# Attention and a channel filter over sixteen images: one channel tile of x replaced by the sum of both

## The chip, the cores and the metric

The kernel runs on one core of one Trainium2 chip. The metric is the time of one execution in device microseconds (us), as the median of several runs. The engines are TensorE (PE, its weight loads apart as PEld), VectorE (DVE), ScalarE (ACT), GpSimd (POOL) and SyncE (SP), which issues DMAs.

## The reference

x is 16 images of 256 channels and 32 x 32 pixels. Each image goes through a self-attention block and then a filter over channels.

```python
theta = einsum('bchw,kc->bkhw', x, theta_w)            # 32 channels, 1024 pixels
phi   = pool2(einsum('bchw,kc->bkhw', x, phi_w))       # 32 channels, 256 pixels
g     = pool2(einsum('bchw,kc->bkhw', x, g_w))         # 128 channels, 256 pixels
beta  = softmax(einsum('bnk,bkm->bnm', theta, phi))    # 1024 x 256
o     = einsum('bchw,kc->bkhw', einsum('bcm,bnm->bcn', g, beta), o_w)
a     = gamma * o + x
out   = a + einsum('fc,bchw->bfhw', tpl, a)            # tpl: circulant, 27 taps over channels
```

tpl is symmetric and circulant, so 1 + tpl is one 256 x 256 matrix whose two diagonal 128 x 128 blocks are equal and whose two other blocks are equal and non-zero only in two corners of 13 channels.

## The kernel before

The 256 channels lie in two tiles of 128 partitions (t or f, 0 and 1), the pixels in two halves of 512 (h). Everything is done in fp32 precision by splitting a number into a high part that TensorE takes in its fast format (fp32r) and a low part that is the rest; `three` multiplies high by high, high by low and low by high. For one image TensorE does, for each half: the theta and phi projections (`theta_phi`, 4 matmuls of 512 columns), the g projection (`g_projection`, 6), the scores (`scores`, 4 of 256 columns), the transposed scores (`scores_transposed`, 2), attention times g (`attention_input_high` 4, `attention_input_low` 2), and the output in PSUM for each tile f: `filter_x` (three matmuls by the diagonal block of the band and one, the corner product of line 1096, by the corner of the other block with the 26 edge channels of the other tile, stacked in `x_edge`), then `add_high_attention` (2) and `add_low_attention` (1) with the weights o_w folded with the band (`w2`).

The work is pipelined over images in an order written out by hand in each engine's queue: `image(i, par)` is image 2i + par, and a queue does the last parts of that image between the first parts of the next one (ni, npar) and the loads and splits of the next but one. Every engine does its own list strictly in order and waits on semaphores. Images 0 and 1 are special cases; the rest run in a hardware loop over pairs, the last pair again written out.

VectorE's list for one image, with the lines of the profile: `sum_thetaphi` of half 0 of the next image (L709), `pool_phi` (L702), `gT_low` (L748), `theta_low` (L715), `pool_g` (L702), the sum of half 1 (L709), `pool_phi`, `split_phi` (two casts L735, one subtraction L737), `theta_low`, `pool_g`, `maxima` of half 0 (L777), `o_in_low` of half 0 (L757), `maxima` of half 1, then

```python
out_of_psum(i, par, 0, 1)
o_in_high(i, par, 1)
out_of_psum(i, par, 0, 0)
o_in_low(i, par, 1)
shifts(ni, npar)
turn_shifts(ni, npar)
for h in range(2):
    spread_shifts(ni, npar, h)
```

`out_of_psum` copies an output half tile from PSUM to `y` (L765 on VectorE, L557 on ScalarE). `shifts` (L782 and two more) makes the softmax shift from the maxima and the logarithms of the sums; `turn_shifts` (L809) transposes it and `spread_shifts` (L817) writes it into `theta_aug`, which `scores_transposed` reads.

ScalarE's list after the probabilities of an image (`probabilities_high` L542, `probabilities` L537) ends so:

```python
o_in_high(i, par, 0)
for h in range(2):
    exp_sums(ni, npar, h)
ln_sums(ni, npar)
x_high(i + 1, par, 1)
for f in (1, 0):
    out_of_psum(i, par, 1, f)
take_thetaphi_rest(i + 1, par, 0)
```

`exp_sums` (L526, four exponentials of 256 columns with a sum) waits for `maxima` of its half, `ln_sums` (L532) for nothing outside, and `shifts` on VectorE waits for `ln_sums`. `x_high` (L504) rounds a half of the next but one image. GpSimd makes the low parts: `prob_low` (L457) for both halves of the attention, the second after `theta_low` of half 1, and `x_low` (L450). SyncE loads x in halves (L306), stores y (L362) and copies the edge channels into `x_edge` (six DMAs, L332).

## Time and profile before

| | |
|---|---|
| time, median of 3 runs | 272.98 us (272.94 to 273.1) |
| profiled execution, span from first to last instruction | 271.3 us |
| PE busy | 265.4 us, 98% |
| DVE busy | 245.9 us, 91% |
| ACT busy | 243.2 us, 90% |
| POOL busy | 149.6 us, 55% |

No separate time is listed for the profiled execution. Its span is 1.7 us under the median of the runs, and that difference stands for what lies around the span. In a timeline a row gives the start, the time, the engine, the line, the operation with its shapes and how many are merged; the bracket at the end is the engine's idle time ahead of it and what ended it. Matmuls are pipelined, so the distance of two starts is what one costs.

### The profile page before, as it was taken

Reading aid. Unit: us, or ns where it says so; the run is one execution under the profiler, and the core shown is the slowest. Engines: PE = TensorE matmul, PEld = TensorE weight load, DVE = VectorE, ACT = ScalarE, POOL = GpSimd, SP = SyncE. Lnnn points to the kernel's source line nnn. Section 1 sums busy time; section 2 is a strip of 40 time slices with the busy share of each in tenths; the row PEclk is TensorE's granted clock in tenths of the full one; section 3 lists DMA queues with packets and bytes.
Section 4 is the critical chain, followed back from the end, with each engine's and each line's share of the span. In section 5 each row is a group of like instructions: output and inputs, shape, how many; then the busy total and the mean of one; then the engine's idle time right before and its main releaser. Section 6 shows DMA issues by size and latency. Waiting matters only on the chain.

```text
span 271.3 us, 4464 instructions
## 1 busy us (share of the span) xinstructions
PE 265.4 (98%) x1196; PEld 211.8 (78%) x1196; DVE 245.9 (91%) x456; ACT 243.2 (90%) x533; POOL 149.6 (55%) x79
## 2 busy tenths in 40 slices
PE   7999999999999999999999999999999999999994
PEld 3576778888888888888888888888887888888873
DVE  4998999999999999999999999999999999999953
ACT  4999999999999999998999999999999989998772
POOL 1585747574565747546673764667466475745100
PEclk9999999999999999999999999999999999999999
DMA  7978085582847657284673828467283855317044
GB/s 198 270 208 212 23 234 169 175 223 81 193 142 225 180 170 182 88 218 149 203 201 144 180 79 246 157 197 206 98 182 124 234 169 172 77 71 178 1 157 155
DMA packets 17380, 44.57 MB, mean 164 GB/s; under 512 B 2654, under 2 KB 3578, under 8 KB 16122
## 3 DMA queue, kind: packets, MB, share of 16 engines
q1 hardware_dynamic: 16682, 44.00, 56.4%
q10 hardware_dynamic: 688, 0.46, 0.5%
q8 instruction: 4, 0.07, 0.1%
q14 instruction: 6, 0.05, 0.1%
HBM read 17.45 MB, written 16.78 MB: 126 GB/s over the span
## 4 chain that ended last, share of the span: by engine, by line
PE 94%; DVE 2%; DMA 2%; ACT 0%; issue 0%; SPq 0%
PE psY L1009 10%; PE psY L988 8%; PE psY L990 7%; PE psY L989 7%; PE psV L1128 6%; PE psY L1112 6%; PE psY L1128 5%; PE psV L1112 5%; PE psV L988 3%; PE psV L990 3%; PE psV L989 3%; PE psX L1066 3%; PE psV L1096 3%; PE psV L1133 3%; PE psZ L1066 3%; PE psY L1118 3%
## 5 line engine op out<-in xcount | busy, mean ns | idle before, releaser
L457 POOL TENSOR_TENSOR prob_lo<-prob,prob_hi 128x1024 fp32r<-128x1024 f32 x30 | 72.1, 2404 | 59.7 <-ACT prob L537 32.5
L450 POOL TENSOR_TENSOR x_lo<-x_raw,x_hi 128x1024 fp32r<-128x1024 f32 x30 | 72.0, 2399 | 35.5 <-ACT x_hi L504 34.0
L504 ACT CAST x_hi<-x_raw 128x1024 fp32r<-128x1024 f32 x30 | 31.5, 1052 | 6.8 <-PE psY L1096 5.2
L526 ACT ACTIVATE psX<-psX,neg_max 128x256 f32<-128x256 f32 x60 | 26.7, 445 | 3.0 <-DVE neg_max L777 3.0
L526 ACT ACTIVATE psZ<-psZ,neg_max 128x256 f32<-128x256 f32 x60 | 27.4, 468 | 0.0
L709 DVE TENSOR_TENSOR thetaphi<-psY,thetaphi_rest 64x512 f32<-64x512 f32 x30 | 20.5, 682 | 3.8 <-ACT thetaphi_rest L508 3.1
L988 PE MATMUL psY<-x_hi,g_hi_w 128*128 128x512 f32 x56 | 22.2, 396 | 0.0
L990 PE MATMUL psY<-x_hi,g_lo_w 128*128 128x512 f32 x56 | 22.0, 393 | 0.0
L989 PE MATMUL psY<-x_lo,g_hi_w 128*128 128x512 f32 x56 | 22.0, 392 | 0.0
L715 DVE TENSOR_TENSOR theta_aug<-thetaphi,theta_aug 32x512 fp32r<-32x512 f32 x30 | 20.5, 683 | 0.9
L702 DVE TENSOR_REDUCE phi_pool<-thetaphi 32x128 f32<-32x512 f32 x30 | 20.2, 674 | 1.0
L702 DVE TENSOR_REDUCE g_pool<-psY 128x128 f32<-128x512 f32 x28 | 19.4, 692 | 0.9
L508 ACT COPY thetaphi_rest<-psY 64x512 f32<-64x512 f32 x30 | 17.5, 583 | 1.7 <-PE psY L1009 0.5
L1009 PE MATMUL psY<-x_hi,tp_w 128*128 128x512 f32 x60 | 18.9, 396 | 0.0
L777 DVE TENSOR_REDUCE neg_max<-psX 128x4 f32<-128x1024 f32 x15 | 18.3, 1217 | 0.6 <-PE psX L1050 0.6
L1009 PE MATMUL psY<-x_lo,tp_w 128*128 128x512 f32 x60 | 18.8, 394 | 0.0
L817 DVE TENSOR_TENSOR theta_aug<-psZ,own_tile 16x512 fp32r<-16x512 f32 x28 | 17.9, 678 | 0.5
L777 DVE TENSOR_REDUCE neg_max<-psZ 128x4 f32<-128x1024 f32 x15 | 18.2, 1213 | 0.0
L513 ACT CAST theta_aug<-thetaphi 32x512 fp32r<-32x512 f32 x30 | 18.1, 602 | 0.0
L519 ACT CAST theta_aug<-thetaphi 32x512 fp32r<-32x512 f32 x30 | 17.2, 617 | 0.4
L542 ACT ACTIVATE prob_hi<-psZ 128x1024 fp32r<-128x1024 f32 x16 | 16.4, 1027 | 0.4
L542 ACT ACTIVATE prob_hi<-psX 128x1024 fp32r<-128x1024 f32 x16 | 16.5, 1032 | 0.1
(189 smaller groups left out, 766.1 us busy)
## 6 DMA issues: line engine op xcount, KB each, us to landing
x_raw<-x SPq DMA_DIRECT2D x30, 512.0 KB, 5.1
out<-y SPq DMA_DIRECT2D x15, 1024.0 KB, 4.0
x_edge<-x_hi SPq DMA_DIRECT2D x64, 104.0 KB
x_edge<-x_lo SPq DMA_DIRECT2D x32, 104.0 KB
x_raw<-x SPq DMA_DIRECT2D x4, 256.0 KB, 4.5
out<-y SPq DMA_DIRECT2D x3, 256.0 KB, 2.1
band_rev<-ring SPq DMA_DIRECT2D x2, 128.0 KB, 6.9
out<-y ACTq DMA_DIRECT2D x1, 256.0 KB, 2.6
```

The costliest lines, as they stand in the source:

```text
L450: nc.gpsimd.tensor_tensor(x_lo[:, par, :, cols], x_raw[:, par, :, cols], x_hi[:, par, :, cols].bitcast(F32), ALU.subtract).then_inc(x_lo_r ...
L457: nc.gpsimd.tensor_tensor(prob_lo[:, h], prob[:, h], prob_hi[:, h].bitcast(F32), ALU.subtract).then_inc(prob_lo_ready, 1)
L504: nc.scalar.copy(x_hi[:, par, :, cols], x_raw[:, par, :, cols]).then_inc(x_hi_ready[h], 1)
L526: last = nc.scalar.activation(tiles[:, t, :], tiles[:, t, :], ACT.Exp, bias=neg_max[:, col:col + 1], accum_out=exp_sum[:, col:col + 1])
L542: nc.scalar.activation(prob_hi[:, h], scores_ps[h][:, :, :], ACT.Exp).then_inc(prob_hi_ready, 1)
L702: return nc.vector.tensor_reduce(dst.rearrange("p (r c) -> p r c", c=SIDE // 2), src.rearrange("p (r a c b) -> p r c a b", a=2, b=2, c=SID ...
L777: nc.vector.tensor_reduce(neg_max[:, h * NT:(h + 1) * NT], tiles, AXIS.X, ALU.max, negate=True).then_inc(neg_max_ready, 1)
L988: nc.tensor.matmul(dst, wh, vh, start=first, stop=False)
L989: nc.tensor.matmul(dst, wh, vl, start=False, stop=False)
L990: return nc.tensor.matmul(dst, wl, vh, start=False, stop=last)
L1009: last = nc.tensor.matmul(thetaphi_bank(i, par, h), tp_w[:, t].rearrange("p a k -> p (a k)"), part[:, par, t, cols], start=part is x_hi an ...
L1112: nc.tensor.matmul(o_in_bank(i, par, h), g_part[:, t, :], prob_hi[:, h, t, :], start=t == 0 and g_part is gT_hi, stop=False)
```

## The change

From the third image on, x's tile 0 is overwritten in `x_raw` by u = x0 + x1 before it is split. The weights of the projections' second tile become the difference of both tiles' weights. Output tile 1 is built from the corner product with u and a diagonal block minus the corner block with x1. In the PSUM of tile 0 stands the sum of both output tiles, from a diagonal block plus the corner block with u alone, with no corner product, and VectorE gets output tile 0 by subtracting tile 1, already in `y`, from it (`rest_of_sum`).

So `filter_x` of tile 0 has three matmuls for four; `stack_edges` copies one tile of edges for two in the same six DMAs; GpSimd gets `add_tiles` twice per image and some one-time weight preparation; ScalarE evacuates tile 1 of both halves, the first between the two `exp_sums`; VectorE does `rest_of_sum` of both halves, the second between the two `spread_shifts`. The loop runs over one pair fewer and the last two pairs are written out. The core of the diff:

```diff
+            def add_tiles(i, par, h):
+                cols = slice(h * HALF, (h + 1) * HALF)
+                pool.wait_ge(x_loaded[h][par], 16 * (i + par))
+                nc.gpsimd.tensor_tensor(x_raw[:, par, 0, cols], x_raw[:, par, 0, cols], x_raw[:, par, 1, cols], ALU.add).then_inc(u_ready[h], 1)
...
             def x_high(i, par, h):
-                act.wait_ge(x_loaded[h][par], 16 * (i + par))
-                if not is_second(i, par):
+                if is_second(i, par):
+                    act.wait_ge(x_loaded[h][par], 16)
+                else:
+                    act.wait_ge(u_ready[h], from_third(1, i, par, 1))
                     act.wait_ge(x_used[h], upto(2, i, par, -2))
...
                 o_in_high(i, par, 0)
-                for h in range(2):
-                    exp_sums(ni, npar, h)
+                exp_sums(ni, npar, 0)
+                out_of_psum(i, par, 0, 1)
+                exp_sums(ni, npar, 1)
                 ln_sums(ni, npar)
                 if has_next_but_one(i, par):
                     x_high(i + 1, par, 1)
-                for f in (1, 0):
-                    out_of_psum(i, par, 1, f)
+                out_of_psum(i, par, 1, 1)
...
+            def rest_of_sum(i, par, h):
+                cols = slice(h * HALF, (h + 1) * HALF)
+                dve.wait_ge(out_evacuated[h][1], upto(1, i, par, 1))
+                dve.wait_ge(out_done[h][0], upto(1, i, par, 1))
+                dve.wait_ge(y_stored[par], 16 * i)
+                nc.vector.tensor_tensor(y[:, par, 0, cols], out_bank(i, par, h, 0), y[:, par, 1, cols],
+                                        ALU.subtract).then_inc(out_evacuated[h][0], 1)
...
                 maxima(ni, npar, 1)
-                out_of_psum(i, par, 0, 1)
                 o_in_high(i, par, 1)
-                out_of_psum(i, par, 0, 0)
+                if is_raw(i):
+                    out_of_psum(i, par, 0, 0)
+                else:
+                    rest_of_sum(i, par, 0)
                 o_in_low(i, par, 1)
                 shifts(ni, npar)
                 turn_shifts(ni, npar)
-                for h in range(2):
-                    spread_shifts(ni, npar, h)
+                spread_shifts(ni, npar, 0)
+                if is_raw(i):
+                    out_of_psum(i, par, 1, 0)
+                else:
+                    rest_of_sum(i, par, 1)
+                spread_shifts(ni, npar, 1)
...
-                three(out_bank(i, par, h, f), (band_hi[:, f, cols], band_lo[:, f, cols]), x_parts(par, f, h), True, False)
+                last = three(out_bank(i, par, h, f), diagonal_parts, x_parts(par, f, h), True, False)
+                if f == 0 and not is_raw(i):
+                    last.then_inc(x_used[h], 1)
+                    return
```

`is_raw` is true for images 0 and 1. In GpSimd's list of image n, `add_tiles` of image n + 3 stands behind each `x_low` of image n + 2. In the last image TensorE finishes tile 1 of each half ahead of tile 0, ScalarE copies tile 1, VectorE subtracts, and the store of half 1, tile 0 is issued by SyncE. Ahead of the loop GpSimd also makes the differences and sums of the weights (`projection_difference` and its parts, `w2_high`, `w2_sum`, `band_combined` and its parts), 13 small operations.

## Rows read from the trace of the kernel before

**Rows 1.** Profile page, parts 1 and 2: TensorE busy, its granted clock.

```profile
PE 265.4 (98%) x1196; PEld 211.8 (78%) x1196; DVE 245.9 (91%) x456; ACT 243.2 (90%) x533; POOL 149.6 (55%) x79
...
PEclk9999999999999999999999999999999999999999
```

**Rows 2.** Windows of one image each, fifteen images: busy us, sum and mean.

```profile
sum 240.72, PE 240.51 PEld 195.75 DVE 226.82 ACT 224.08 POOL 141.92; mean PE 16.03 PEld 13.05 DVE 15.12 ACT 14.94 POOL 9.46
```

**Rows 3.** Timeline of TensorE: start us, us, what; g projection, scores.

```profile
130.12 0.40 PE L988 MATMUL psY<-x_hi,g_hi_w 128*128 128x512 f32 x1
...
137.06 0.64 PE L1050 MATMUL psX<-phi_aug,theta_aug 96*128 96x256 f32 x4
```

**Rows 4.** Timeline of VectorE: start us, us, what, idle before and its releaser.

```profile
46.97 0.17 DVE L782 TENSOR_TENSOR psZ<-neg_max,psZ 128x8 f32<-128x8 f32 x1
...
130.28 0.68 DVE L709 TENSOR_TENSOR thetaphi<-psY,thetaphi_rest 64x512 f32<-64x512 f32 x1 [0.21 <-ACT thetaphi_rest L508]
...
132.87 0.69 DVE L702 TENSOR_REDUCE g_pool<-psY 128x128 f32<-128x512 f32 x1
133.62 0.68 DVE L709 TENSOR_TENSOR thetaphi<-psY,thetaphi_rest 64x512 f32<-64x512 f32 x1
...
135.04 0.97 DVE L735 CAST phi_aug<-phi_pool 32x256 fp32r<-32x256 f32 x2
...
137.81 1.22 DVE L777 TENSOR_REDUCE neg_max<-psX 128x4 f32<-128x1024 f32 x1
...
139.54 1.21 DVE L777 TENSOR_REDUCE neg_max<-psZ 128x4 f32<-128x1024 f32 x1
...
142.59 0.68 DVE L757 TENSOR_TENSOR o_in_lo<-psY,o_in_hi 128x512 fp32r<-128x512 f32 x1
143.19 0.16 DVE L782 TENSOR_TENSOR psZ<-neg_max,psZ 128x8 f32<-128x8 f32 x1
...
144.72 1.28 DVE L817 TENSOR_TENSOR theta_aug<-psZ,own_tile 16x512 fp32r<-16x512 f32 x2
...
255.56 0.16 DVE L782 TENSOR_TENSOR psZ<-neg_max,psZ 128x8 f32<-128x8 f32 x1
```

**Rows 5.** Timeline of ScalarE, the same image.

```profile
139.06 0.45 ACT L526 ACTIVATE psX<-psX,neg_max 128x256 f32<-128x256 f32 x1 [0.21 <-DVE neg_max L777]
...
140.87 0.46 ACT L526 ACTIVATE psZ<-psZ,neg_max 128x256 f32<-128x256 f32 x1
...
142.84 0.18 ACT L532 ACTIVATE psZ<-exp_sum 128x8 f32<-128x8 f32 x1
...
144.49 0.59 ACT L557 COPY y<-psV 128x512 f32<-128x512 f32 x1
144.97 0.59 ACT L557 COPY y<-psY 128x512 f32<-128x512 f32 x1
```

**Rows 6.** Timeline of GpSimd: one half tile at the start, then the same image.

```profile
7.95 1.26 POOL L407 TENSOR_TENSOR x_lo<-x_raw,x_hi 128x512 fp32r<-128x512 f32 x1 [5.86 <-ACT x_hi L563]
...
133.14 2.40 POOL L457 TENSOR_TENSOR prob_lo<-prob,prob_hi 128x1024 fp32r<-128x1024 f32 x1 [2.24 <-ACT prob L537]
...
144.53 2.40 POOL L450 TENSOR_TENSOR x_lo<-x_raw,x_hi 128x1024 fp32r<-128x1024 f32 x1 [2.51 <-ACT x_hi L504]
```

**Rows 7.** Source line 735 (casts of pooled phi), min/median/max ns, over two images.

```profile
L735 DVE CAST phi_aug<-phi_pool x4: 285/454/649, 135.0 to 151.7; 32x256 fp32r<-32x256 f32 x4
```

**Rows 8.** Timeline of SyncE's queue: the two loads of x in this image.

```profile
136.81 0.96 SPq L306 DMA_DIRECT2D x_raw<-x  x2
```

**Rows 9.** Source line 306 (loads of x), landing times of two images' loads.

```profile
DMA to landing us min/median/max: 4.3/4.9/5.4
```

**Rows 10.** Profile page, part 6: the last stores, KB, us to landing.

```profile
out<-y SPq DMA_DIRECT2D x3, 256.0 KB, 2.1
...
out<-y ACTq DMA_DIRECT2D x1, 256.0 KB, 2.6
```

More of the change, by code:

```diff
@@ L241, in over_images @@
             image(0, 1)
-            with engine.Fori(1, PAIRS - 1) as i:
+            with engine.Fori(1, PAIRS - 2) as i:
                 image(i, 0)
                 image(i, 1)
-            image(PAIRS - 1, 0)
-            image(PAIRS - 1, 1)
+            for i in (PAIRS - 2, PAIRS - 1):
+                image(i, 0)
+                image(i, 1)
         def is_number(i):
@@ L255, in has_next_but_one, with has_next_but_two, is_raw @@
             return not (is_number(i) and i == PAIRS - 1)
+        def has_next_but_two(i, par):
+            return not is_number(i) or 2 * i + par + 3 < B
+        def is_raw(i):
+            return is_number(i) and i == 0
         def is_last(i, par):
@@ L336, in x_edges @@
                     sp.wait_ge(x_lo_ready[h], from_second(1, i, par, 1))
-                stack_edges(x_edge[:, par], x_edge_loaded[par], (x_hi[:, par], x_hi[:, par], x_lo[:, par]))
+                tiles = slice(0, CT if is_raw(i) else 1)
+                high, low = x_hi[:, par, tiles], x_lo[:, par, tiles]
+                stack_edges(x_edge[:, par, tiles], x_edge_loaded[par], (high, high, low))
             def image0():
@@ L481, in image @@
                 if has_next(i, par):
-                    for h in range(2):
-                        pool.wait_ge(theta_lo_ready, upto(2, *following(i, par), h + 1))
-                        prob_low(i, par, h)
-                if has_next_but_one(i, par):
-                    for h in range(2):
-                        x_low(i + 1, par, h)
+                    pool.wait_ge(theta_lo_ready, upto(2, *following(i, par), 1))
+                    prob_low(i, par, 0)
+                    if is_second(i, par):
+                        add_tiles(1, 1, 1)
+                    pool.wait_ge(theta_lo_ready, upto(2, *following(i, par), 2))
+                    prob_low(i, par, 1)
+                for h in range(2):
+                    if has_next_but_one(i, par):
+                        x_low(i + 1, par, h)
+                    if is_second(i, par) and h == 0:
+                        band_combined_parts()
+                    if has_next_but_two(i, par):
+                        ni, npar = following(i, par)
+                        add_tiles(ni + 1, npar, h)
             over_images(pool, image)
@@ L671, in image @@
                 o_in_high(i, par, 0)
-                for h in range(2):
-                    exp_sums(ni, npar, h)
+                exp_sums(ni, npar, 0)
+                out_of_psum(i, par, 0, 1)
+                exp_sums(ni, npar, 1)
                 ln_sums(ni, npar)
@@ L955, in image @@
                     for h in range(2):
-                        out_of_psum(i, par, h, 0)
+                        rest_of_sum(i, par, h)
                     return
@@ L1126, in add_high_attention @@
                 pe.wait_ge(o_in_hi_ready[h], upto(1, i, par, 1))
-                for w2_part in (w2_hi, w2_lo):
-                    nc.tensor.matmul(out_bank(i, par, h, f), w2_part[:, cols], o_in_hi[:, h, :], start=False, stop=False)
+                parts = (w2_hi[:, cols], w2_lo[:, cols]) if f == 1 or is_raw(i) else (w2_hi_s[:], w2_lo_s[:])
+                for w2_part in parts:
+                    nc.tensor.matmul(out_bank(i, par, h, f), w2_part, o_in_hi[:, h, :], start=False, stop=False)
             def add_low_attention(i, par, h, f):
@@ L1266, in image @@
                     for h in range(2):
-                        for f in range(CT):
+                        for f in (1, 0):
                             add_high_attention(i, par, h, f)
-                        for f in range(CT):
+                        for f in (1, 0):
                             add_low_attention(i, par, h, f)
```

96 lines of the change are left out of this document (85 added, 11 removed).

## The prediction

> **What bounds the kernel now.** I read the busy shares first: TensorE is busy 98% of the span and its granted clock is the full 2.4 GHz in every slice [rows 1]. The windows of one image each, from the second to the last but one, give TensorE 16.03 us of busy time per image and no idle, while VectorE (15.12) and ScalarE (14.94) come within 7% of it [rows 2]. So TensorE sets the pace, and two others are close behind. A busy share hides how close, so I went through the timelines of one image, engine by engine. VectorE starts `shifts` at 46.97 and 255.56 for the first and the last of fourteen such points [rows 4]: thirteen periods of 16.05 us.
>
> The reader should look at VectorE's gaps: in the whole image it is idle for 0.21 us ahead of the sum of half 0, and for some 0.15 us ahead of the sum of half 1, which starts 0.75 us after `pool_g` though an operation with nothing to wait for follows after 0.60 (142.59 to 143.19) [rows 4]. VectorE therefore needs about 15.7 us of its 16.05. And there is one handover that is just in time: `shifts` starts at 143.19, when VectorE has done four operations of 0.6 us since the maxima of half 1 (139.54 + 1.21); the logarithm it needs ended on ScalarE at 142.84 + 0.18 = 143.02 [rows 4, 5]. The slack there is 0.13 us once a handoff of 0.04 is allowed.
>
> **The change, part by part.** *TensorE loses two matmuls per image.* From the g projection (130.12) to the scores (137.06) stand 30 matmuls' worth of 512 columns: 6.94 us, 0.231 each [rows 3]. Two fewer in each of 14 images are 6.5 us, and the image would take 15.58 us if TensorE still set the pace. That is the whole gain on offer.
>
> *ScalarE gets a copy between the two `exp_sums`, and loses one at the end of its list.* Two copies in a row start 0.48 us apart (144.49, 144.97) [rows 5]. The sum over the image is unchanged, but the place isn't: it lies between the maxima of half 0 and the logarithm. ScalarE starts the first exponential at 139.06, 0.03 us after the maxima end (137.81 + 1.22), the first of half 1 at 140.87 with nothing between, the logarithm at 142.84 [rows 4, 5]. All of that is a chain, and the copy lengthens it by 0.48.
>
> *VectorE loses a copy ahead of `shifts` and gets a subtraction behind the first `spread_shifts`.* `rest_of_sum` reads PSUM and SBUF and writes 128 x 512, the form of `o_in_low` at 142.59, which takes 0.68 and lets the next one start after 0.60 [rows 4]. So VectorE has 0.6 us less to do while it waits for the logarithm and 0.6 us more afterwards.
>
> Both moves hit the same circle: maxima of half 0, exponentials, copy, exponentials, logarithm, `shifts`, transposes, spread, subtraction, spread, sum of the image after, and everything down to the next maxima. It lies in strict queues, so it can't be shorter than its links. In us:
>
> maxima of half 0 to first exponential 1.25; to the logarithm 3.78; the new copy 0.48; the logarithm and its handoff 0.18 + 0.04; `shifts` to the first spread 1.53 (143.19 to 144.72); first spread to subtraction 0.60; subtraction to second spread 0.60; second spread to the next sum 0.71. Together 9.17 [rows 4, 5].
>
> Then from the sum of half 0 to the maxima of half 0. It took 7.53 (130.28 to 137.81) [rows 4], with two waits in it. One is the 0.15 named above, for ScalarE's copy of the rest of theta and phi; ScalarE now comes there one copy (0.48) earlier, so it goes. The other is in the casts: of the same form of 32 x 256 the slowest takes 649 ns and the quickest 285 [rows 7]. The slow one starts at 135.04 and ends at 135.69, and GpSimd's `prob_low` ran until 133.14 + 2.40 = 135.54 [rows 4, 6]: the cast stood behind it. `prob_low` waits for ScalarE's exponentials, which also come 0.48 earlier against the sum, so it would end some 4.8 us after the sum where the cast starts 4.6 after it, and the block shrinks from 0.36 to about 0.05. That leaves 7.53 - 0.15 - 0.31 = 7.07. TensorE's side of the same stretch must allow it: the g projection starts when the subtraction has freed its bank, 0.53 before the sum, and 29 matmuls of 0.231, the scores (0.64) and a handoff of 0.1 end 6.9 after it. It does, barely. I take 7.09.
>
> The Trainium skill ("SBUF — State Buffer", Who interferes with whom) says that a cast in VectorE's two-port mode and a GpSimd instruction lock each other out for the whole of one instruction; by this rule, the trace agrees, since the cast ends 0.15 us after GpSimd's subtraction and not before.
>
> The new period is 9.17 + 7.09 = 16.26 us. Before, by the same links, the circle was 9.17 - 0.48 - 0.60 + 7.53 = 15.62, well hidden under TensorE's 16.05. Now it is 0.68 above the 15.58 that TensorE would need. The waits seen before go; the new one is VectorE's at `shifts`: it gets there three operations after the maxima of half 1, about 1.84 us, and the logarithm comes 0.95 us later.
>
> *GpSimd adds the tiles.* A half tile of the same form took 1.26 us [rows 6], so 2.5 us per image on an engine with 9.46 busy of 16 [rows 2]. The first add stands ahead of the second `x_low`, where GpSimd was idle for 2.51 us; the second ahead of `prob_low`, with 2.24 us idle [rows 6]. Both gaps hold 1.26. The load that the first add needs is issued 6.5 us after the sum (136.81) and lands 4.3 to 5.4 us later, by 12.0 [rows 8, 9]; the add is due by 14.0. Cost nothing; if it is late by more than 1 us, `x_low` and what follows are late by the rest.
>
> *SyncE* issues as many DMAs, those of the edges half as large: nothing, or a little earlier. *The weight preparation* is thirteen small GpSimd operations, most of them in idle stretches at the start; the adds delay the second `x_high` of image 2 by about 0.6 us and a transpose by 0.4, of which VectorE feels 0.1. *The loop* with one pair fewer costs nothing that the rows show.
>
> **The sum, against the profiled span of 271.3.** Start +0.1. The first period (images 1 to 2) still ends in the old subtraction-free list but has ScalarE's copy: +0.5. Thirteen periods: 13 x (16.26 - 16.05) = +2.7. The tail: the last image's second spread is 0.6 later behind the subtraction, one corner product is gone (-0.23), and the last output is now a subtraction that has to follow ScalarE's copy (0.04 + 0.68), which starts one matmul sooner (-0.23); against that SyncE's store lands in 2.1 where ScalarE's took 2.6 [rows 10]. Together +0.3 to +0.8, I take +0.6. Sum +3.9, span 275.2, time 272.98 + 3.9 = 276.9.
>
> **The rivals.**
> *A: the circle is as said but without relief.* If ScalarE's earlier arrival doesn't bring `prob_low` forward, or the copy costs its full 0.59, the stretch to the maxima stays between 7.38 and 7.53 and the period is 16.55 to 16.8: 13 x 0.5 to 0.75 + 1.2, time 280.7 to 284. For it: this stretch has never been seen with another phase of GpSimd. Against: the quick cast is in the same rows.
>
> *B, faster: the logarithm is hidden after all.* Then TensorE sets the pace again, 15.58 us, and the time is 272.98 - 13 x 0.47 + 1.0 = 267.9. It decides at `shifts`: the chain through ScalarE would have to be 0.68 us shorter than its rows. Eight exponentials of 0.45 us make most of it [rows 5], and nothing in the new order takes one away.
>
> *C: GpSimd becomes part of the circle.* If the second add slips past 1.8 us after the sum, `theta_low` with two inputs in SBUF meets it, and `prob_low` starts late as well. A slip of 0.6 us is 0.6 us of VectorE's path: period 16.9, time about 285. For it: 0.9 us of slack only, and a load may land late. Against: landing times are within 1.1 us of each other [rows 9].
>
> The same page and section of the Trainium skill says that a VectorE instruction with two SBUF inputs waits for a GpSimd instruction that reads SBUF; no row here shows it, and by it every add that meets `theta_low` would cost up to its length.
>
> *D: no change*, a period of 16.0 to 16.1 with start and tail cancelling it: nothing speaks for it but the closeness of 16.26 and 16.05.
>
> **How the numbers follow.** Forecast 0.65; A 0.16; C 0.05; B 0.07; D 0.07, of which I give 0.04 to a time within 0.2% (about 0.55 us, what a measurement of this kernel can tell from no change). The likeliest case's own range is a period of 16.15 to 16.45 with ends of +0.9 to +1.5: 275.2 to 279.7. Reaching into A and D, 274.3 to 281.5 leaves out B, C, the worst of A. Slower 0.88, same 0.04, faster 0.08.
>
> **What would show it.** Right: TensorE's busy share falls to about 94% and idle time appears on it; VectorE's `shifts` (the subtraction of 8 columns) shows an idle of about 0.9 us per image released by ScalarE's logarithm; the chain of waits runs through exponentials and VectorE; the slow cast shortens. Wrong: no idle ahead of `shifts`; a period of 15.6; idle ahead of `x_hi` released by GpSimd (C); or a granted clock at 1.2 GHz in some slice, which no row of before shows and which isn't in the sum.

## The result

The changed kernel takes 287.69 us (median of 4 runs, 287.55 to 288.08) against 273.03 us before (4 runs): a ratio of 1.054, 95% interval 1.0525 to 1.0555. The forecast was 276.9 us with a range of 274.3 to 281.5. The sign was right and the time lies 6 us above the range.

The profile page of the kernel after, its busy times, TensorE's granted clock, the chain that ended last, and the adds of GpSimd (busy us and mean ns, then idle ahead):

```profile
PE 270.8 (95%) x1168; PEld 202.3 (71%) x1168; DVE 252.2 (88%) x456; ACT 245.8 (86%) x533; POOL 191.0 (67%) x120
...
PEclk9999999999999999999999999999999999999999
...
DVE 58%; ACT 21%; issue 13%; PE 5%; DMA 1%; DVEq 1%; SPq 0%
...
L510 POOL TENSOR_TENSOR x_raw<-x_raw 128x512 f32<-128x512 f32 x28 | 36.6, 1306 | 0.0
```

TensorE's busy share fell from 98% to 95%, and its matmuls are 28 fewer. Its clock is at the 2.4 GHz level in every slice, as before [rows 1], so the clock has no part in the difference. The chain of waits runs through VectorE and ScalarE, with 5% for TensorE. The adds (L510) are 28 of 1.31 us, and had no idle time ahead.

The waits, us in total, times, longest:

```profile
POOL prob_lo L516 <- DVE theta_aug L792: 48.3, 27, 2.9
...
DVE psZ L868 <- ACT psZ L609: 8.9, 14, 0.7
...
DVE o_in_hi L830 <- PE psY L1220: 3.6, 14, 0.3
```

and one of the waits before:

```profile
POOL prob_lo L457 <- DVE theta_aug L715: 27.2, 15, 2.4
```

VectorE waits at `shifts` for the logarithm in each of 14 images. That was forecast. Before, GpSimd waited for `theta_low` ahead of the second `prob_low` of an image only, 15 times; ahead of the first it waited for ScalarE's exponential [rows 6]. After, it waits for `theta_low` 27 times, ahead of both. That was not forecast.

**Where the 14.0 us of span went.** From image 1 on `shifts` runs once per image (image 0 has its own, at 17.91 before and 18.11 after), so its starts cut the trace into start, first period, thirteen periods and tail. "First `shifts`" is that of image 1. The starts in the trace after are 32.85, 50.69 and, for the last, 269.06; the same row of before stands in [rows 4], and its first is at 31.20:

| | before | after | measured | forecast |
|---|---|---|---|---|
| first `shifts` | 31.20 | 32.85 | +1.65 | +0.1 |
| first period | 15.77 | 17.84 | +2.07 | +0.5 |
| thirteen periods | 13 x 16.045 | 13 x 16.80 | +9.8 | +2.7 |
| tail | 15.74 | 16.24 | +0.5 | +0.6 |

The span grew by 14.0 us and the time by 14.7; the remaining 0.7 lies outside the span.

The timeline of VectorE after (start us, us, what, idle before and its releaser), one circle from `shifts` of an image to the next but for the middle of the list:

```profile
134.83 0.17 DVE L868 TENSOR_TENSOR psZ<-neg_max,psZ 128x8 f32<-128x8 f32 x1 [0.66 <-ACT psZ L609]
...
136.38 0.68 DVE L903 TENSOR_TENSOR theta_aug<-psZ,own_tile 16x512 fp32r<-16x512 f32 x1
137.09 0.69 DVE L850 TENSOR_TENSOR y<-psY,y 128x512 f32<-128x512 f32 x1
137.81 0.68 DVE L903 TENSOR_TENSOR theta_aug<-psZ,own_tile 16x512 fp32r<-16x512 f32 x1
138.53 0.68 DVE L786 TENSOR_TENSOR thetaphi<-psY,thetaphi_rest 64x512 f32<-64x512 f32 x1
...
140.41 0.68 DVE L792 TENSOR_TENSOR theta_aug<-thetaphi,theta_aug 32x512 fp32r<-32x512 f32 x1
...
143.14 0.89 DVE L812 CAST phi_aug<-phi_pool 32x256 fp32r<-32x256 f32 x2
...
145.83 1.22 DVE L863 TENSOR_REDUCE neg_max<-psX 128x4 f32<-128x1024 f32 x1
...
151.57 0.17 DVE L868 TENSOR_TENSOR psZ<-neg_max,psZ 128x8 f32<-128x8 f32 x1 [0.60 <-ACT psZ L609]
```

ScalarE's timeline of the same image: the exponential of the probabilities that `prob_low` reads, the first exponential of `exp_sums`, the new copy and the logarithm:

```profile
139.77 1.01 ACT L614 ACTIVATE prob<-psX 128x1024 f32<-128x1024 f32 x1
...
147.08 0.45 ACT L603 ACTIVATE psX<-psX,neg_max 128x256 f32<-128x256 f32 x1 [0.39 <-DVE neg_max L863]
...
148.90 0.60 ACT L634 COPY y<-psY 128x512 f32<-128x512 f32 x1
...
151.36 0.18 ACT L609 ACTIVATE psZ<-exp_sum 128x8 f32<-128x8 f32 x1
```

GpSimd's timeline of the same image:

```profile
141.17 2.40 POOL L516 TENSOR_TENSOR prob_lo<-prob,prob_hi 128x1024 fp32r<-128x1024 f32 x1 [1.69 <-DVE theta_aug L792]
```

Link by link against the forecast: `shifts` to the first spread 1.55 (forecast 1.53); spread, subtraction, spread, sum 0.71, 0.72, 0.72 (forecast 0.60, 0.60, 0.71); sum to maxima 7.30 here and 7.47 in the next image (forecast 7.09); maxima to the first exponential 1.25 (1.25); to the logarithm 4.28 (4.26; the copy 0.46 of it from start to start); logarithm to `shifts` 0.21 (0.22). The thirteen periods are not alike: in eight of them sum to maxima takes 7.30 to 7.32, in the other five, all in the loop, 7.46 or 7.47. The mean period is 0.54 us longer than forecast: 0.24 in the spacing around the subtraction, and 0.28 on average between sum and maxima.

### The profile page after: what moved, and what is told of

It is laid out like the page before. It is cut to its first block, busy times and chain, and to the rows that moved or that the text cites. A ratio compares the mean times of both kernels' runs of the same rounds, so it can differ in the third digit from the quotient of the medians.

```text
span 285.3 us, 4390 instructions
## 1 busy us (share of the span) xinstructions
PE 270.8 (95%) x1168; PEld 202.3 (71%) x1168; DVE 252.2 (88%) x456; ACT 245.8 (86%) x533; POOL 191.0 (67%) x120
## 3 DMA queue, kind: packets, MB, share of 16 engines
HBM read 17.45 MB, written 16.78 MB: 120 GB/s over the span
## 4 chain that ended last, share of the span: by engine, by line
DVE 58%; ACT 21%; issue 13%; PE 5%; DMA 1%; DVEq 1%; SPq 0%
ACT psZ L603 9%; ACT psX L603 8%; DVE g_pool L779 8%; DVE theta_aug L792 7%; DVE thetaphi L786 7%; DVE neg_max L863 6%; DVE phi_pool L779 5%; DVE phi_aug L812 5%; DVE psZ L895 4%; DVE theta_aug L903 4%; ACT y L634 3%; DVE gT_lo L825 2%; DVE y L850 2%; DMA x_raw<-x 1%; ACT psZ L609 1%
## 5 line engine op out<-in xcount | busy, mean ns | idle before, releaser
L510 POOL TENSOR_TENSOR x_raw<-x_raw 128x512 f32<-128x512 f32 x28 | 36.6, 1306 | 0.0
L903 DVE TENSOR_TENSOR theta_aug<-psZ,own_tile 16x512 fp32r<-16x512 f32 x28 | 19.1, 683 | 0.9
L1161 PE MATMUL psX<-theta_aug,phi_aug 112*128 112x512 f32 x32 | 11.7, 446 | 5.4 <-DVE theta_aug L903 5.4
L614 ACT ACTIVATE prob<-psZ 128x1024 f32<-128x1024 f32 x16 | 16.2, 1015 | 0.0
L614 ACT ACTIVATE prob<-psX 128x1024 f32<-128x1024 f32 x16 | 16.2, 1012 | 0.0
L812 DVE CAST phi_aug<-phi_pool 32x256 fp32r<-32x256 f32 x28 | 14.0, 498 | 0.9
```

The source lines that it names most:

```text
L510: nc.gpsimd.tensor_tensor(x_raw[:, par, 0, cols], x_raw[:, par, 0, cols], x_raw[:, par, 1, cols], ALU.add).then_inc(u_ready[h], 1)
L614: nc.scalar.activation(prob[:, h], scores_ps[h][:, :, :], ACT.Exp).then_inc(prob_ready, 1)
L903: nc.vector.tensor_tensor(rows[:, tiles, :], row, own_rows(tiles), ALU.mult).then_inc(shift_rows_ready, 1)
```

## The experiments

Periods are read from the starts of `shifts`, as above. The medians of before beside these runs are 273.15 to 273.31 us.

| run | time, us | ratio to before, 95% | first `shifts` | first period | mean of 13 periods |
|---|---|---|---|---|---|
| after | 287.69 | 1.054 (1.0525 to 1.0555) | 32.85 | 17.84 | 16.80 |
| e1, evacuation order alone | 284.34 | 1.0396 (1.0353 to 1.044) | 31.40 | 16.26 | 16.80 |
| e2, fewer corners alone | 268.96 | 0.9855 (0.9805 to 0.9904) | 31.27 | 15.76 | 15.73 |
| e3, w2 low from PSUM | 286.48 | 1.0496 (1.0444 to 1.0549) | 32.01 | 17.98 | 16.79 |
| e4, adds of 16 columns | 285.64 | 1.0446 (1.0402 to 1.0489) | 33.46 | 16.35 | 16.80 |
| e5, `prob_low` not held | 283.65 | 1.0364 (1.0322 to 1.0406) | 32.94 | 17.82 | 16.53 |
| e6, evacuations as before | 272.13 | 0.9954 (0.9931 to 0.9977) | 33.10 | 17.34 | 15.72 |
| e7, VectorE copies tile 1 | 280.75 | 1.0264 (1.0218 to 1.0309) | 33.16 | 17.35 | 16.32 |
| e9, subtraction behind both spreads | 288.43 | 1.0533 (1.0487 to 1.0578) | 34.23 | 17.82 | 16.90 |
| e10, three repairs | 278.05 | 1.017 (1.0146 to 1.0194) | 32.11 | 17.50 | 16.19 |
| e11, before, `prob_low` not held | 273.15 | 0.9996 (0.9981 to 1.0011) | 31.02 | 15.78 | 16.04 |
| e12, subtraction into rows 96 on | 284.27 | 1.0395 (1.0367 to 1.0423) | 33.02 | 17.83 | 16.58 |
| e13, subtraction into rows 0 on | 287.26 | 1.0504 (1.0475 to 1.0533) | 34.32 | 17.83 | 16.79 |

The column of the first `shifts` is less sure than the others, since single executions start up to 1.5 us later: e13's profiled execution took 288.55 us where the other six took 287.03 to 287.70, and e9's and e4's are the slowest of their runs too. All of this lies ahead of image 0's `shifts` (19.58 in e13, 18.11 after). From there to image 1's it is 13.26 to 13.29 us in before, e1, e2 and e11, and 14.74 or 14.75 after and in e5, e6, e7, e9, e12 and e13. It is 14.59 in e4, 13.69 in e3 and 13.70 in e10.

### e1: the order of evacuations, and nothing else

```diff
 (kernel before, ScalarE)
                exp_sums(ni, npar, 0)
+               out_of_psum(i, par, 0, 1)
                exp_sums(ni, npar, 1)
...
-               for f in (1, 0):
-                   out_of_psum(i, par, 1, f)
+               out_of_psum(i, par, 1, 1)
 (VectorE)
                maxima(ni, npar, 1)
-               out_of_psum(i, par, 0, 1)
...
                spread_shifts(ni, npar, 0)
+               out_of_psum(i, par, 1, 0)
                spread_shifts(ni, npar, 1)
```

> The kernel before with one part of the change alone: ScalarE copies tile 1 of half 0 between the two exp_sums and tile 1 of half 1 at the end, VectorE copies tile 0 of half 0 where it did and tile 0 of half 1 between the two spread_shifts. No adds, no subtraction, all corner products kept; the output is the reference's. Theory 1, the circle through ScalarE and VectorE sets the period: the links as they stand in the trace of after (16.8 us) depend on this order alone, so thirteen periods of 16.8 for 16.05 are +9.8, the first +0.5, the end +0.6: about 284 us. Theory 2, the adds on GpSimd are what slows the changed kernel: this one stays at TensorE's pace, 273 to 274 us.

284.34 us. No adds, no subtraction, no combined weights, all corner products in place, and the period is 16.80, that of the whole change. So the order of the evacuations alone makes the thirteen periods, and two matmuls more or fewer per image don't show in them. VectorE's timeline of e1:

```profile
131.80 0.17 DVE L782 TENSOR_TENSOR psZ<-neg_max,psZ 128x8 f32<-128x8 f32 x1 [0.65 <-ACT psZ L532]
...
133.34 0.68 DVE L817 TENSOR_TENSOR theta_aug<-psZ,own_tile 16x512 fp32r<-16x512 f32 x1
134.06 0.69 DVE L765 COPY y<-psY 128x512 f32<-128x512 f32 x1
134.78 0.68 DVE L817 TENSOR_TENSOR theta_aug<-psZ,own_tile 16x512 fp32r<-16x512 f32 x1
```

The idle ahead of `shifts` is much as after (0.51 to 0.67 in the 14 images for 0.60 to 0.71), and a plain copy between the spreads has the same 0.72 on both sides as the subtraction. The first period is 16.26, 0.49 above before: that term of the forecast (+0.5) was right for what it counted, the copy.

### e2: fewer corner products, and nothing else

```diff
 (kernel before, filter_x of tile f)
-                three(out_bank(i, par, h, f), ...)
+                last = three(out_bank(i, par, h, f), ...)
+                raw = is_number(i) and i == 0
+                if f == 0 and not raw:
+                    last.then_inc(x_used[h], 1)
+                    return
```

The corner product of output tile 0 is left out from the third image on, and so is not part of its output.

> The kernel before with the two corner products of output tile 0 left out from the third image on (tile 0 of the output lacks the corner block's part) and nothing else. Theory 1, VectorE's list is right behind TensorE: the period falls from 16.05 only to VectorE's 15.7, 13 x 0.35 = 4.5 us, time about 268.5. Rival, TensorE stays the bound: 15.58 us, time about 266.8 us. If the time falls by under 2 us, something else holds the image.

268.96 us, period 15.73: 4.2 us less than the 273.18 beside it, with no adds and no subtraction. That is what the missing corner products give in this order of evacuations. The period stays 0.15 above the 15.58 forecast for TensorE, near the first theory's 15.7. But VectorE isn't shown to set it. TensorE is busy 15.70 of 15.70 us in the windows of three images of e2 (which doesn't make it the bound either, as it is busy 16.26 of 16.29 in e7), and VectorE's list has small gaps left: in the image that ends with the `shifts` at 141.49, 0.70 us from `pool_g` to the sum of half 1 and 1.22 from the maxima of half 1 to the copy, where e7 has 0.60 and 1.13. The 15.7 was itself too high, for the same reason. It left out a wait in the timeline of VectorE before:

```profile
140.79 0.69 DVE L765 COPY y<-psY 128x512 f32<-128x512 f32 x1
```

This copy starts 1.25 us after the maxima of half 1 (139.54 [rows 4]), for 1.13 in e7. So the agreement with 15.7 may be luck, and what holds the image at 15.73 stays open.

### e6: everything but the evacuations

The four evacuations of an image are plain copies at their old places: the lines that e1's diff adds are taken out of the changed kernel, and those that it takes out are put back. The subtraction is left out, so output tile 0 holds the sum of both tiles from the third image on.

> The changed kernel with the four evacuations back in their places of before, as plain copies: VectorE copies both tiles of half 0, ScalarE both of half 1. The subtraction is left out, so tile 0 of the output holds the sum from the third image on. Adds, weights, edges and TensorE's work as changed. Theory 1, the circle: period 15.75 us, VectorE's own list as in the run with fewer corners, so 13 x (16.80 - 15.75) = 13.7 us less, 0.5 less in the first period and 0.6 at the end: 272.9 us, the rest over that run being the start and the first period. Theory 2, GpSimd's adds or its locks hold a good part of the period: over 276 us.

272.13 us, period 15.72. With adds, combined weights and halved edges in place the thirteen periods are those of e2. So the adds cost nothing in a steady image of this order. Start and first period (+1.9 and +1.6 against before) eat most of the gain.

### e4: adds of 16 columns

```diff
 (add_tiles)
-                cols = slice(h * HALF, (h + 1) * HALF)
+                cols = slice(h * HALF, h * HALF + 16)
```

The other 496 columns of each half keep x's tile 0, so the output isn't the reference's from the third image on.

> The changed kernel with each add on GpSimd cut from 512 columns to 16, so that tile 0 of x is x0 but for 16 columns of each half (the output is wrong from the third image on); all waits and the order stay. Theory 1, the circle: the period stays at 16.8, only the first, where a cast of VectorE stood behind an add, gets about 1 us shorter: 286.5 us. Theory 2, the adds slow the steady image: the period falls towards 16.26 or below, time under 281 us.

285.64 us. The thirteen periods don't move (16.80). The first period falls from 17.84 to 16.35, 1.49 us. What the adds did there stands in the timeline of VectorE after, in the first period:

```profile
38.06 0.95 DVE L792 TENSOR_TENSOR theta_aug<-thetaphi,theta_aug 32x512 fp32r<-32x512 f32 x1
...
41.07 2.08 DVE L812 CAST phi_aug<-phi_pool 32x256 fp32r<-32x256 f32 x2
```

and in that of GpSimd after, beside it:

```profile
38.02 0.45 POOL L497 TENSOR_TENSOR band_c<-band 128x128 f32<-128x128 f32 x1
38.43 0.90 POOL L498 TENSOR_TENSOR band_c<-band 128x128 f32<-128x128 f32 x1
...
41.66 1.34 POOL L510 TENSOR_TENSOR x_raw<-x_raw 128x512 f32<-128x512 f32 x1
```

The pair of casts that starts at 41.07 takes 2.08 us. It ends at 43.15, just after GpSimd's add, which ran from 41.66 to 43.00. `theta_low` at 38.06 takes 0.95 where 0.68 is usual, beside the first `band_c`. In e4 the same instructions take 0.88 and 0.68, together 1.47 less, nearly all of the 1.49. GpSimd is blocked in turn: its second `band_c`, which stood next to `theta_low`, took 0.90 here and 0.47 in e4.

### e3: the low part of w2 from PSUM

```diff
-                nc.vector.tensor_tensor(w2_lo[:], w2_raw[:], w2_hi[:].bitcast(F32), ALU.subtract)
+                nc.vector.scalar_tensor_tensor(w2_lo[:], w2_ps, gamma_sb[:, 0:1], w2_hi[:].bitcast(F32),
+                                               ALU.mult, ALU.subtract)
```

> The changed kernel, with w2's low part made from PSUM as before (one input in SBUF) and not from two tensors in SBUF. Theory, the 2.25 us of that operation in the trace of after (0.47 before) is a wait behind GpSimd's prob_low: it takes 0.47 again and the time falls by about 1.7 us to 286.0. Rival, it waits for data or for the longer way of w2 through GpSimd: the time stays at 287.7, and the 2 us appear elsewhere.

286.48 us, 1.2 less than after. The timeline of VectorE after, where `w_lo` is made from two tensors in SBUF:

```profile
20.85 2.25 DVE L980 TENSOR_TENSOR w_lo<-w_raw,w_hi 128x256 fp32r<-128x256 f32 x1
```

GpSimd's timeline after, at the same time:

```profile
20.44 2.39 POOL L516 TENSOR_TENSOR prob_lo<-prob,prob_hi 128x1024 fp32r<-128x1024 f32 x1 [0.34 <-ACT prob L614]
```

VectorE's timeline of e3, where one of the two inputs is in PSUM:

```profile
21.07 0.47 DVE L980 SCALAR_TENSOR_TENSOR w_lo<-psV,gamma_sb,w_hi 128x256 fp32r<-128x256 f32 x1
...
23.47 1.38 DVE L792 TENSOR_TENSOR theta_aug<-thetaphi,theta_aug 32x512 fp32r<-32x512 f32 x1
```

With both inputs in SBUF the subtraction of 256 columns takes 2.25 us: it began 0.4 us after GpSimd's `prob_low` and ended 0.27 after it. With one in PSUM it takes 0.47 beside the same `prob_low`. But from image 0's `shifts` to image 1's it is only 1.05 less (13.69 for 14.74; image 1's came 0.84 earlier, as this execution started later). `theta_low` (two SBUF inputs) at 23.47 took 1.38 instead of 0.68: it began inside GpSimd's add, which ran from 23.02 to 24.30. The wait is passed in part to the next instruction of that kind. Another 0.14 comes back in the first period (17.98 for 17.84).

### e5: `prob_low` of half 0 no longer waits for `theta_low`

```diff
 (kernel after, GpSimd)
-                    pool.wait_ge(theta_lo_ready, upto(2, *following(i, par), 1))
                     prob_low(i, par, 0)
```

> The changed kernel without GpSimd's wait for theta_low of half 0 ahead of prob_low of half 0; it still waits for both exponentials. In the trace of after, prob_low starts 2.6 to 2.8 us after the sum, released by theta_low, while the exponentials were done 2.25 after it. The prediction had it start 2.4 after the sum and the cast of phi freed by that. If only that wait holds it, prob_low starts 0.2 to 0.4 earlier, the cast's wait shrinks by as much, and 13 periods give 13 x 0.2 to 0.3 = 3 to 4 us: 284 us. Rival, GpSimd and theta_low (both with two inputs in SBUF) exclude each other anyway: either prob_low starts when theta_low ends, and the time stays within 0.5 us of 287.7, or it comes first and theta_low waits for it, which would be up to 2 us per image slower.

283.65 us: 4.0 us less than after, of which 13 x 0.27 = 3.5 in the periods. GpSimd's timeline of e5:

```profile
139.49 2.44 POOL L516 TENSOR_TENSOR prob_lo<-prob,prob_hi 128x1024 fp32r<-128x1024 f32 x1 [1.46 <-ACT prob L613]
```

VectorE's timeline of e5:

```profile
137.09 0.68 DVE L785 TENSOR_TENSOR thetaphi<-psY,thetaphi_rest 64x512 f32<-64x512 f32 x1
...
138.97 0.68 DVE L791 TENSOR_TENSOR theta_aug<-thetaphi,theta_aug 32x512 fp32r<-32x512 f32 x1
...
141.71 0.68 DVE L811 CAST phi_aug<-phi_pool 32x256 fp32r<-32x256 f32 x2
...
144.19 1.22 DVE L862 TENSOR_REDUCE neg_max<-psX 128x4 f32<-128x1024 f32 x1
```

The rest of the probabilities starts 2.40 us after the sum, where it started 2.64 after. It ends 4.84 after the sum, the casts shrink from 0.89 to 0.68, and from sum to maxima it takes 7.10. The forecast had 4.8 and 7.09. So the arithmetic of that stretch was right for a kernel without this wait. The difference between the images is gone too: all thirteen periods are 16.51 to 16.54, where after has five of 16.89 and eight of 16.72 to 16.75.

### e11: the same edit to the kernel before

```diff
 (kernel before, GpSimd)
-                    pool.wait_ge(theta_lo_ready, upto(2, *following(i, par), h + 1))
+                    if h == 1:
+                        pool.wait_ge(theta_lo_ready, upto(2, *following(i, par), h + 1))
                     prob_low(i, par, h)
```

> The kernel before, whole and with the right output, with one edit: GpSimd takes the rest of half 0's probabilities without waiting for theta_low of half 0. Theory 1 (TensorE's list of 16.03 us sets the pace before, VectorE's follows it): shorter casts only make VectorE wait elsewhere, 272.4 to 273.4 us, period 16.0 to 16.05. Theory 2 (VectorE sets the pace, with TensorE only equally long): 0.2 to 0.27 us less an image, 269.5 to 270.5 us.

273.15 us, ratio 0.9996 (0.9981 to 1.0011). The timeline of GpSimd shows why it can't tell the two theories apart:

```profile
132.97 2.40 POOL L457 TENSOR_TENSOR prob_lo<-prob,prob_hi 128x1024 fp32r<-128x1024 f32 x1 [2.19 <-ACT prob L538]
```

`prob_low` starts 2.84 us after the sum (130.13), as it did before (133.14 and 130.28, [rows 4, 6]), and what ends its wait is ScalarE's exponential in both. The wait for `theta_low` was in the code before, and cost nothing, because ScalarE came later. This run says only that.

### e7: VectorE copies tile 1 of half 0

```diff
 (kernel after, ScalarE)
                 exp_sums(ni, npar, 0)
-                out_of_psum(i, par, 0, 1)
                 exp_sums(ni, npar, 1)
 (VectorE)
                 maxima(ni, npar, 1)
+                out_of_psum(i, par, 0, 1)
                 o_in_high(i, par, 1)
```

> The changed kernel, whole and with its output right, but VectorE copies tile 1 of half 0 ahead of o_in_high as before, and ScalarE has no copy between the exponentials. Theory 1: the circle through ScalarE falls to 16.3 us, VectorE's own list rises to 7.39 + 5.38 + 3.69 = 16.46 us and sets the period: 13 x 0.34 + 0.4 = 4.8 us less, 282.9 us, with no idle ahead of shifts. Rival, the place of the copy doesn't matter, only how much VectorE has to do: the time rises by up to 13 x 0.6 = 8 us.

280.75 us, period 16.32, and no idle ahead of `shifts`. The whole computation, one copy more on VectorE and one fewer on ScalarE, is 6.9 us faster than after. The circle through the exponentials is no longer the bound; VectorE's own list is. It came out 2.2 us below the 282.9 expected, which summed that list too long.

### e9: the subtraction behind both spreads

```diff
                 spread_shifts(ni, npar, 0)
+                spread_shifts(ni, npar, 1)
                 if is_raw(i):
                     out_of_psum(i, par, 1, 0)
                 else:
                     rest_of_sum(i, par, 1)
-                spread_shifts(ni, npar, 1)
```

> The changed kernel with the subtraction of half 1 behind both spread_shifts and not between them. In the trace of after the three start 0.72 us apart, where the prediction had 0.60; the two spreads in a row were 0.60 apart before. If the interleaving costs 0.12 each way, the period falls by 0.12 to 0.24, unless the g projection, whose bank is freed 0.6 us later, brings the scores in late (by the links 0.16 later than the maxima could start): 285.5 to 287.0. If nothing changes, the spacing belongs to the operations and not to their order.

288.43 us, no gain. The timeline of VectorE of e9:

```profile
136.68 0.17 DVE L868 TENSOR_TENSOR psZ<-neg_max,psZ 128x8 f32<-128x8 f32 x1 [0.38 <-ACT psZ L609]
...
138.22 1.28 DVE L903 TENSOR_TENSOR theta_aug<-psZ,own_tile 16x512 fp32r<-16x512 f32 x2
139.54 0.69 DVE L850 TENSOR_TENSOR y<-psY,y 128x512 f32<-128x512 f32 x1
140.15 0.67 DVE L786 TENSOR_TENSOR thetaphi<-psY,thetaphi_rest 64x512 f32<-64x512 f32 x1
...
147.78 1.22 DVE L863 TENSOR_REDUCE neg_max<-psX 128x4 f32<-128x1024 f32 x1 [0.26 <-PE psX L1145]
```

TensorE's timeline of e9, at the g projection:

```profile
140.28 0.50 PE L1079 MATMUL psY<-x_hi,g_hi_w 128*128 128x512 f32 x1 [0.59 <-DVE y L850]
```

From `shifts` to the sum it is 3.47 us for 3.70 after: the two spreads are 0.60 apart again. But the subtraction frees the bank of the g projection 0.6 us later, counted from `shifts`, TensorE waits 0.59 for it, and the maxima come 7.63 after the sum with a wait for the scores in front. The gain is given back, and more.

### e12 and e13: where the subtraction writes

Left open by e1 and e9: why an instruction between the spreads costs 0.72 us on either side. In e12 the subtraction of half 1 has 32 partitions and writes rows 96 to 127 of y, in e13 the same 32 partitions and rows 0 to 31.

```diff
-                nc.vector.tensor_tensor(y[:, par, 0, cols], out_bank(i, par, 1, 0), y[:, par, 1, cols],
-                                        ALU.subtract)
+                nc.vector.tensor_tensor(y[96:128, par, 0, cols], out_bank(i, par, 1, 0)[0:32], y[0:32, par, 1, cols],
+                                        ALU.subtract)      # e13: y[0:32, par, 0, cols]
```

> The changed kernel with the subtraction between the two spreads cut to 32 partitions and written to rows 96 to 127 of y, the rows where the spreads write in theta_aug (the output of half 1, tile 0 is therefore not computed from the third image on; the rest is). Theory 1 (VectorE starts an instruction before the one ahead of it has ended only if both write from the same rows on; the spreads write from row 96 on, the sums, casts and copies from row 0 on, and 0.71 us is the price of each change): spread, subtraction and second spread start 0.60 us apart, the next sum 0.71 after; the circle is 0.24 us shorter, period 16.55 us, time 284.2 to 284.8 us. Theory 2 (0.72 us is the price of an instruction of another kind or size between the spreads, wherever it writes): spacing 0.72 and 0.72, period 16.80, time 287.2 to 288.0 us. The Trainium skill ("VectorE: DVE Perf Modes", Two Vector instructions with no wait between them) has a rule of this kind: an instruction whose inputs or output start in another group of 32 partitions than the last ones starts only when all earlier ones have finished.

> The control of the run before it: the same subtraction of 32 partitions, written to rows 0 to 31 of y, where it belongs (the other rows of half 1, tile 0 are not computed from the third image on). Both theories: spacing 0.72 and 0.72 around it, period 16.80 us, time 287.2 to 288.0 us. If it is at 284.5 us as well, the size of the instruction sets the spacing and both are wrong.

VectorE's timeline of e12:

```profile
152.08 0.68 DVE L911 TENSOR_TENSOR theta_aug<-psZ,own_tile 16x512 fp32r<-16x512 f32 x1
152.69 0.67 DVE L849 TENSOR_TENSOR y<-psY,y 32x512 f32<-32x512 f32 x1
153.29 0.67 DVE L911 TENSOR_TENSOR theta_aug<-psZ,own_tile 16x512 fp32r<-16x512 f32 x1
153.99 0.68 DVE L786 TENSOR_TENSOR thetaphi<-psY,thetaphi_rest 64x512 f32<-64x512 f32 x1
```

and of e13:

```profile
154.57 0.68 DVE L911 TENSOR_TENSOR theta_aug<-psZ,own_tile 16x512 fp32r<-16x512 f32 x1
155.29 0.68 DVE L849 TENSOR_TENSOR y<-psY,y 32x512 f32<-32x512 f32 x1
156.00 0.69 DVE L911 TENSOR_TENSOR theta_aug<-psZ,own_tile 16x512 fp32r<-16x512 f32 x1
156.72 0.68 DVE L786 TENSOR_TENSOR thetaphi<-psY,thetaphi_rest 64x512 f32<-64x512 f32 x1
```

One instruction, one size, another row to write to: the starts are 0.61, 0.60 and 0.70 apart in e12 and 0.72, 0.71 and 0.72 in e13. The times differ by 3.0 us (284.27 and 287.26), the 13 x 0.24 expected. `spread_shifts` writes `theta_aug` from row 96 on (three blocks of 32 rows stand ahead of it), the subtraction, the copies and the sums write from row 0 on. Where the start row of the output changes from one instruction to the next, the second starts only when the first has ended. `theta_low` writes from row 64 on, and from it to the next instruction it is 0.71 or 0.72 us in before, after, e1, e5 and e12. By the same reading these are changes of rows that the kernel before had already; no run takes them out.

The Trainium skill ("VectorE: DVE Perf Modes", Two Vector instructions with no wait between them) says that an instruction whose output starts in another 32-row quadrant than the last output into the same memory is held until all earlier ones have finished. The traces of e12 and e13 agree: 0.70 to 0.72 us at each change of rows, 0.60 to 0.61 without one, for an instruction of 0.67 to 0.69.

### e10: three repairs together

The changed kernel with the edits of e3, e5 and e7.

> The changed kernel, whole and with the right output, with three of the edits measured so far together: VectorE copies tile 1 of half 0 (none between the exponentials), GpSimd takes the rest of half 0's probabilities without waiting for theta_low, and the low part of w2 is made from PSUM again. Theory 1: with the copy alone (280.75 us) VectorE's list set the pace, 16.32 us an image; the freed casts take 0.2 to 0.27 us an image off that list (13 images: 2.6 to 3.5 us) and the weight about 1.2 us off the start: 276.0 to 277.2 us, a period of 16.05 to 16.12, still slower than before. Theory 2: the gains don't add up, because the exponentials are near enough to bind again: 278 to 280 us. Theory 3: TensorE's shorter list shows at last: a period of 15.6 to 15.8, below 273 us.

278.05 us: the best whole version of the change, 9.6 us faster than it and 1.7% slower than before (1.0146 to 1.0194). It lies 0.9 us above the first theory's range, and inside the second's, for another reason than the one given there: there is no idle ahead of `shifts`, so the exponentials don't bind. The period is 16.19 where 16.05 to 16.12 was expected. The casts of an image are 0.67 us for 0.89 and 1.03 in e7, 0.29 less, but 0.16 of that comes back ahead of VectorE's copy. Its timeline in e10:

```profile
143.18 1.21 DVE L861 TENSOR_REDUCE neg_max<-psZ 128x4 f32<-128x1024 f32 x1
144.42 0.69 DVE L840 COPY y<-psY 128x512 f32<-128x512 f32 x1
...
146.82 0.16 DVE L866 TENSOR_TENSOR psZ<-neg_max,psZ 128x8 f32<-128x8 f32 x1
```

TensorE's timeline of e10, the last matmul of tile 1:

```profile
143.99 0.40 PE L1237 MATMUL psY<-o_in_lo,w_hi 128*128 128x512 f32 x1
```

From the maxima to the copy it is 1.24 us (1.33 in the image before) for 1.13 in e7. The copy starts 0.03 us after the matmul that completes tile 1 ends (143.99 + 0.40), and 0.13 after it in the image before. That matmul ends 1.20 to 1.21 us after the maxima start, where it ended 1.02 after them in e7. This speaks for VectorE having caught up with TensorE's order there; no run takes that wait away.

## Why the prediction was right and wrong

**Right: the bound moves off TensorE, into a circle through ScalarE and VectorE.** The idle ahead of `shifts` in all 14 images and the chain of waits show it. That idle is 0.60 to 0.71 where 0.9 was said; 0.20 to 0.31 more is idle ahead of `o_in_high`, three operations earlier, where VectorE waits for TensorE, which the forecast had at nothing. e1 makes the same 16.80 with the order alone, e6 removes it, and e7 breaks it at the copy. The copy between the exponentials cost 0.46 for a forecast 0.48, and exponentials, logarithm and handoffs were as forecast within 0.03. Rival B, where the gain of the corner products shows in the time, didn't occur; only with the evacuations back in their places (e6) does it show in the periods, and then at 15.72 and not 15.58.

**Half right: the gain on offer.** 0.47 us per image for TensorE was forecast; e2 gives 0.31 and stops at 15.73. The forecast put VectorE's need at about 15.7, but the sum for rival B didn't use it and went down to 15.58. What stops the image at 15.73 is not shown (e2).

**Right: the tail,** +0.5 for +0.6, and that the adds cost nothing in a steady image (e4, e6). Rival C didn't occur.

**Wrong: "`prob_low` waits for ScalarE's exponentials, which also come 0.48 earlier against the sum, so it would end some 4.8 us after the sum".** It waits for two things. ScalarE's exponential did come earlier (it ended at 140.78, 2.25 after the sum, for 2.69 before), and then the second wait in the same list, for `theta_low` of half 0, came last: it ended at 141.09, and `prob_low` started at 141.17. In the profile before that wait never showed for half 0, since it ended first; it stands in the code. After, GpSimd is behind `theta_low` for both halves (27 times for 15). So `prob_low` of half 0, which started 2.83 to 2.87 us after the sum before, came forward by 0.2 us (2.64) in eight images and by 0.05 (2.79 or 2.80) in the five others, and not by 0.48. Why it starts 0.08 us after the end of `theta_low` in the one kind and 0.23 in the other stays open. The casts stayed slow (0.89 and 1.04 for 0.97 before [rows 4]). Measured by e5: 0.27 us per image, about 3.5 of the 10.8 us by which the forecast missed. Rival A, which had a chance of 0.16, is near to this: ScalarE's earlier arrival brought `prob_low` forward by little, and the stretch to the maxima took 7.37 on average where A had 7.38 to 7.53. Its time, 280.7 to 284, lacked the two terms that follow.

**Wrong: 0.60 us from spread to subtraction and from subtraction to spread.** They took 0.72 and 0.72, 0.24 us per image and 3.1 in all, by e12 against e13. I took the price of an instruction from a row where the one after it writes from the same row on (142.59 to 143.19 [rows 4]), and charged 0.71 only where the trace had shown it, behind the second spread. That 0.71 was the sign: the spreads write from another row on, and the edit puts an instruction between them.

With both terms the forecast's own sum of a period is 16.26 + 0.24 + 0.28 = 16.78, for 16.80 measured.

**Wrong: start +0.1 and first period +0.5.** They were +1.65 and +2.07, 3.1 us more. The list of small GpSimd operations was costed by what GpSimd has to do, and not by what VectorE does beside it. The change put VectorE instructions with two inputs in SBUF next to GpSimd's long ones (`w_lo` 2.25 for 0.47, e3), and adds next to casts and to `theta_low` (1.47 us in the first period, e4). The prediction said of the rule for two SBUF inputs that no row showed it; the rows of e3 show it now.

The Trainium skill ("SBUF — State Buffer", Who interferes with whom) says that such an instruction and a GpSimd instruction that reads SBUF share a read interface. The trace agrees: `w_lo` ends 0.27 us after `prob_low`, and with one input in PSUM it takes 0.47 us in the same place. It would have been worth a term of its own in the sum: the GpSimd operation beside it, a `prob_low`, is 2.40 us long [rows 6], and that bounds the term.

**Not settled.** The start is 1.65 us later. Of this 1.45 lies between image 0's `shifts` and image 1's (14.74 for 13.29), and there e3's edit takes out 1.05 and e4's 0.15; the remaining 0.25, among the small operations, wasn't taken apart. The 0.20 ahead of image 0's `shifts` is less than what single executions differ by. The 0.7 us by which the time grew beyond the span isn't explained either. A version in which GpSimd does the subtraction of half 1 wasn't tried. Nor was one with the shift rows placed at row 0, which by the reading of e12 would take out the changes of rows around the subtraction.

## What to carry to other kernels

When an edit brings one input of an instruction forward, list all its waits, also those that never showed: the second latest is the new start. Take the price of an instruction from a row with the same neighbours, and where one row in a chain is 0.1 us longer than its like, ask why before putting something next to it. One-time work beside a loop is costed by what it blocks on the other engine, not by its own length.

## What the hardware showed that I had not expected

- VectorE starts an instruction of 512 columns 0.60 us after the one before if both write from the same row on, and 0.70 to 0.72 us after it if the start row changes between 0 and 96 (e12 against e13, the same instruction otherwise).
- A VectorE subtraction with both inputs in SBUF took 2.25 us in place of 0.47 when it started inside a GpSimd subtraction of 2.39 us; with one input in PSUM it was not delayed (e3). Casts of 32 x 256 were delayed in the same way, 2.08 us for two in place of 0.88 (e4). GpSimd is delayed in turn: an operation of 128 x 128 took 0.90 in place of 0.47.
- In e5 `prob_low` started 0.16 us before the end of `theta_low`, which also reads SBUF twice, and took 2.44 us for 2.40, and so in all thirteen images (2.42 to 2.44): an overlap of 0.16 us at the end of an instruction cost at most 0.04.
